# Cross-attention with LayerNorm: slices of x prepared one iteration ahead, and four gaps in the SBUF layout

## The reference

```python
qs = (x @ wq)   ; ks = (ctx @ wk) ; vs = (ctx @ wv)        # split into 16 heads
scores = einsum('bhqd,bhkd->bhqk', qs, ks) / sqrt(32)
scores = where(mask, -inf, scores)
attn = einsum('bhqk,bhkd->bhqd', softmax(scores), vs)
out = attn @ wo + x
return (out - mean(out)) / sqrt(var(out) + 1e-5) * gamma + beta
```

## Time and profile before

| | |
|---|---|
| median of the runs | 677.32 us |
| the profiled execution | 678.04 us, its span in the trace 676.3 us |
| TensorE busy | 616.6 us (91%) |
| VectorE busy | 521.6 us (77%) |
| ScalarE busy | 510.6 us (76%) |
| GpSimd busy | 493.3 us (73%) |
| DMA engines' share | 40.9%, mean 121 GB/s |
| granted clock of TensorE | 0.968 of full speed on average |

### The profile page before, as it was taken

How to read it: one execution, slowest core, us unless ns; L and a number is a source line. 1 busy time by engine, 2 the same in 40 slices (tenths; PEclk the granted TensorE clock), 3 DMA queues, 4 the chain that set the end, 5 groups by cost and what they waited for, 6 DMA issues and landing times.

```text
span 676.3 us, 12773 instructions
## 1 busy us (share of the span) xinstructions
PE 616.6 (91%) x3856; PEld 484.2 (72%) x3856; DVE 521.6 (77%) x1060; ACT 510.6 (76%) x1558; POOL 493.3 (73%) x640
## 2 busy tenths in 40 slices
PE   8999969899898998989899898989989898998995
PEld 6887757777676787767678676767867676777663
DVE  6677757968787786878869687886868878688887
ACT  6788748868787896877779687787868779587851
POOL 4577347867868777786977778697777869667784
PEclk9999979989998998999999899999989999998998
DMA  8522345444544343344434344443434443452102
GB/s 280 160 63 76 103 130 147 119 132 120 136 133 134 102 140 113 116 142 127 139 95 132 100 133 136 116 152 108 131 96 123 138 136 89 130 150 86 44 36 109
DMA packets 60756, 82.02 MB, mean 121 GB/s; under 512 B 22544, under 2 KB 23056, under 8 KB 60688
## 3 DMA queue, kind: packets, MB, share of 16 engines
q1 hardware_dynamic: 60688, 81.21, 40.9%
HBM read 39.53 MB, written 16.78 MB: 83 GB/s over the span
## 4 chain that ended last, share of the span: by engine, by line
PE 57%; DVE 13%; POOL 12%; issue 6%; SPq 5%; ACT 4%; DMA 2%; POOLq 0%; DVEq 0%
PE bank L424 20%; PE bank L523 18%; PE bank L462 6%; PE bank L473 5%; PE bank L496 4%; POOL pn L973 3%; POOL xl L958 3%; DVE pr L782 2%; POOL y L997 2%; DVE nm L788 2%; PE bank L501 2%; SPq L280 2%; PE bank L477 2%; ACT pr L630 2%; POOL pn L975 2%
## 5 line engine op out<-in xcount | busy, mean ns | idle before, releaser
L630 ACT ACTIVATE pr<-pr,nm 128x77 f32<-128x77 f32 x1024 | 270.5, 349 | 59.4 <-DVE nm L788 55.8
L973 POOL TENSOR_TENSOR pn<-pr,rec 128x512 f32<-128x512 f32 x128 | 135.0, 1055 | 126.4 <-DVE rec L797 90.2
L782 DVE SCALAR_TENSOR_TENSOR pr<-msk,bank 128x308 f32<-128x308 uint8 x256 | 109.5, 469 | 83.4 <-PE bank L462 78.1
L424 PE MATMUL bank<-xh,wqh 128*128 128x512 f32 x256 | 108.9, 425 | 43.5 <-POOL xl L958 43.5
L795 DVE TENSOR_REDUCE sm<-pr 128x8 f32<-128x616 f32 x128 | 100.6, 786 | 16.9 <-ACT pr L630 16.3
L424 PE MATMUL bank<-xl,wqh 128*128 128x512 f32 x256 | 106.5, 416 | 0.0
L424 PE MATMUL bank<-xh,wql 128*128 128x512 f32 x256 | 106.0, 414 | 0.0
L788 DVE TENSOR_REDUCE nm<-pr 128x8 f32<-128x616 f32 x128 | 101.8, 795 | 4.4
L462 PE MATMUL bank<-ks,qs 128*128 128x234 f32 (+1 forms) x672 | 103.2, 290 | 2.0 <-DVE pr L782 2.0
L523 PE MATMUL bank<-woh,ah 128*128 128x512 f32 x256 | 103.2, 403 | 1.5 <-DVE al L804 1.4
L601 ACT ACTIVATE ptr<-bank 128x512 f32<-128x512 f32 (+1 forms) x256 | 96.1, 430 | 10.8 <-PE bank L473 10.7
(11 more groups left out here) (85 smaller groups left out, 927.7 us busy)
## 6 DMA issues: line engine op xcount, KB each, us to landing
qs<-qs SPq DMA_DIRECT2D x336, 64.0 KB, 2.0
xraw<-xT SPq DMA_DIRECT2D x58, 256.0 KB, 3.8
xres<-x SPq DMA_DIRECT2D x58, 256.0 KB, 2.7
out<-y SPq DMA_DIRECT2D x56, 256.0 KB, 2.3
ptr<-xT SPq DMA_DIRECT2D x6, 256.0 KB, 9.7
zt<-x SPq DMA_DIRECT2D x6, 256.0 KB, 4.2
out<-zt SPq DMA_DIRECT2D x6, 256.0 KB, 2.0
ks<-khc SPq DMA_DIRECT2D x36, 38.5 KB, 2.0
```

What stands on the lines that cost most here:

```text
L424: last = nc.tensor.matmul(misc_bank(("q", i))[:], w[:, k, m * P:(m + 1) * P], s[:, blk % 2, k, :], start=(k == 0 and n == 0), stop=(k == K ...
L630: last = nc.scalar.activation(s, s, ACT.Exp, bias=nm[:, t % 2, h:h + 1], scale=1.0)
L782: nc.vector.scalar_tensor_tensor(out=pr[:, 4 * g:4 * g + 4, :], in0=msk[:, m % MR, t % 4, :].unsqueeze(1).broadcast_to([P, 4, LK]), scalar ...
L973: nc.gpsimd.tensor_tensor(pn[:, half, 0:4, :].rearrange("p s (e k) -> p (s e) k", e=2), pr[:, hs, 0:KM], rec[:, t % 2, hs].unsqueeze(2).br ...
```

## The change

On SyncE, ScalarE and GpSimd the three steps of a slice are each issued one iteration earlier from iteration 7 on; at the end of iteration 6 each of the three does one slice more than before. TensorE's and VectorE's programs stay as they are. Four unused tensors are declared, and `mhalf` is moved.

```diff
+XDUE = 6
...
         ks = sb("ks", [P, 2, NG, 9, KW], f32r)
+        sb("pad_vm", [P, 16])
         vm = sb("vm", [P, NB, 4, 2, HD])
...
         ident = sb("ident", [P, P])
-        mhalf = sb("mhalf", [P, 1])
+        sb("pad_x", [P, 96])
         xraw = sb("xraw", [P, NX, D])
...
         pr = sb("pr", [P, H, LK])
+        sb("pad_pn", [P, 16])
         pn = sb("pn", [P, 2, 5, P])
...
         msk = sb("msk", [P, MR, 4, LK], u8)
+        mhalf = sb("mhalf", [P, 1])
+        sb("pad_q", [P, 88])
...
             for t in range(T + LAG):                      # SyncE
-                if t >= 1 and t + 9 < 4 * NBLK:
-                    load_slice(t + 9)
+                n = t + 9 + (t > XDUE)
+                if 1 <= t and n < 4 * NBLK:
+                    load_slice(n)
...
                 if t in KS_AT:
                     place_k(*KS_AT[t])
+                if t == XDUE:
+                    load_slice(t + 10)
...
                 if t >= 2:                                # ScalarE
                     keep_pt(t - 2, 1)
-                if 1 <= t and t + 8 < 4 * NBLK:
-                    keep_x(t + 8)
+                n = t + 8 + (t > XDUE)
+                if 1 <= t and n < 4 * NBLK:
+                    keep_x(n)
...
                 exps(t, 1)
+                if t == XDUE:
+                    keep_x(t + 9)
...
                     gain_and_shift(t - LAG - 2)           # GpSimd
-                if t + 8 < 4 * NBLK:
-                    low_x(t + 8)
+                n = t + 8 + (t > XDUE)
+                if n < 4 * NBLK:
+                    low_x(n)
...
                 normalise(t, 0)
+                if t == XDUE:
+                    low_x(t + 9)
```

## The result

The kernel after takes 627.28 us (median of 4 runs, 625.71 to 627.51) against 677.22 us before (4 runs, 676.59 to 677.45). The ratio is 0.9259, 95% interval 0.9243 to 0.9275. The forecast of 630.3 us was 3.0 us too high. The profiled execution took 627.39 us, its span 625.6.

The account below looks back on a forecast made before the run. TensorE, busy 91%, was held mainly by waits for GpSimd's low part of x; 678.04 - 51.2 + 4.2 = 631.0 for the profiled execution, 630.3 us as median, range 622 to 641.

Parts of the forecast that it names:

- the stall: Iterations 3 modulo 4: TensorE's wait for GpSimd's low part of x goes in all 12 blocks, -51.2 us.
- The gaps: Four unused tensors shift operand starts in memory; claimed not to change TensorE's pace, 0 us.
- start-up: Iterations 7 to 9: exponentials wait behind slice 16's late landing, delaying TensorE; +4.2 us, bounds 0 and 7.
- another distance between matmuls: Sign of being wrong: 512-column matmuls on TensorE no longer 233 ns apart from start to start.
- the half clock: TensorE's slow stretches behind 8 of the 12 waits go with them; 8 x 1.57 = 12.5 us of the gain.
- A third plain iteration in a row: Rival: it does not hold in the blocks, 0.8 us come back in each; 640 us, chance 0.14.
- the residual of tile 1: VectorE, start-up: ends at 105.1, so `project_o(2)`, which writes the bank it reads, starts 3.6 us later.
- `low_q(12)`: Iteration 8: frees the bank of `project_q(13)` late, an estimated 0.6 us.
- The first rival: Both operands on a multiple of 128 bytes bring 512-column matmuls from 233 to 213 ns; 620 us, chance 0.07.
- GpSimd's loop: Plain iterations: GpSimd has no idle time, repeats every 8.00 us against TensorE's 8.03, and holds if matmuls get faster.
- The last iterations: From iteration 56 on: same instructions at the same distance, 0, give or take 1.6 us for one slow clock stretch.

Follow-up runs that it names:

- e10: Kernel after with weights at 160 and x and attention at 416 modulo 512, some other gaps changed too; 623.21 us in one execution.
- e6: Kernel after with x and attention at 0 modulo 512 instead of 384, weights still at 128; 629.79 us, ratio 0.9313 to the kernel before.
- the later hand-over: Kernel after with the slices ahead from iteration 10 on instead of 7; 622.56 us, ratio 0.9211 to the kernel before.

## Why the prediction was right, step by step

The term that makes up nearly all of the change, the stall, was right for the reason given. The gaps were put at nothing and were not nothing, and in the start-up the size came out by a path that was not the one followed. One of the prediction's own signs of being wrong came: another distance between matmuls.

*The stall.* Right in mechanism and size. The slices alone took the 12 blocks from 477.93 to 426.77 us, 51.2 less; predicted were 426.7 and 51.2. The trace of before has the 8 slow stretches in these blocks that the prediction had worked out from the mean clock; with the slices alone none is left there, so the half clock went with the waits. How the 51.2 divide was less exact: 38.7 us were called waiting, and the earlier trace rows has 35.9. A third plain iteration in a row held at 8.04, so that rival fell.

*Start-up.* The size was right for the slices alone: iteration 8 started at 105.11 instead of 100.90, +4.2, as predicted, and iteration 10 still had it (124.61 against 120.40). The path was another than I followed, and that the size fits to 0.1 us is luck. I had `project_o(2)` wait for the residual of tile 1 and added 0.6 us for `low_q(12)`; neither shows as a wait of TensorE. In fact it waited for ScalarE's `keep_pt`, which stood behind the two late slices and frees the bank of the transposes. ScalarE in order of time after, the answer to the earlier trace rows:
```profile
92.05 0.63 ACT L610 ACTIVATE xh<-xraw 128x512 fp32r<-128x512 f32 x1 [7.77 <-DMA xraw<-xT]
92.59 0.58 ACT L610 ACTIVATE qs<-bank 128x512 fp32r<-128x512 f32 x1
93.07 0.76 ACT L610 ACTIVATE ptr<-bank 128x512 f32<-128x512 f32 x2
99.25 0.63 ACT L610 ACTIVATE xh<-xraw 128x512 fp32r<-128x512 f32 x1 [5.43 <-DMA xraw<-xT]
99.79 0.80 ACT L662 ACTIVATE y<-z,rs 128x512 f32<-128x512 f32 x1
100.49 2.09 ACT L639 ACTIVATE pr<-pr,nm 128x77 f32<-128x77 f32 x8
102.49 0.73 ACT L610 ACTIVATE ptr<-bank 128x512 f32<-128x512 f32 x2
```
The exponentials start at 100.49 (I had 101.4), and the transposes at 103.37 wait for the `ptr` copy at 102.49. I read only what stands behind `keep_x(16)` and left out `keep_pt(5, 1)` and `keep_pt(6, 0)`, which stand behind the slices in the same queue. Iteration 8 starts 4.6 us behind the start of `keep_x(16)`, in the kernel after (99.25) as with the slices alone (100.50); the slice came 1.25 us earlier in the kernel after, and so that one has +3.0 and not +4.2. There the pause was followed by another slow stretch of the clock, 0.50 from 104.20 to 107.62, and that is why its iteration 8 takes 9.54 us: its `project_o` starts its matmuls 0.44 us apart.
```profile
104.97 0.65 PE L532 MATMUL bank<-woh,ah 128*128 128x512 f32 x1
105.41 0.63 PE L532 MATMUL bank<-wol,ah 128*128 128x512 f32 x1
```

*The gaps.* The term that was mis-sized: 0 predicted, about -5 us measured. The distances say the same: 3.5 and 4.1 ns less in the two projections, 768 times each, are 5.8 us if TensorE sets the pace throughout. The range from 622 to 641 had room for a term of this size. From the two groups in the earlier trace rows I concluded that no start matters, since they ran at one pace with opposite operands off the multiple. Both have the same difference of 96 between their operands' starts, modulo 256, and it is the difference that counts, so the comparison could not show it. The first rival had the sign, but of its 20 ns per matmul 3.5 to 4.1 came, and 4.4 and 5.8 in e10; what the rest of the distance above 213 ns is, no run shows. Its condition, both operands on a multiple of 128, was not the one either: e6 has it and 232.6 ns.

*GpSimd's loop.* I had its 8.00 us as a floor for a plain iteration. It was not: TensorE runs at 7.96 after and at 7.89 in e10. GpSimd needs longer than that (8.04) and falls back, but three plain iterations in a row did not use up its lead.

*The last iterations.* From iteration 56 to the end of the span 97.47 us before, 97.06 after, 95.9 with the slices alone, where the clock had one slow stretch instead of three: within the 1.6 that was allowed.

The sum for the profiled execution after: +3.0 to iteration 8, -53.3 in the 12 blocks, -0.4 behind them, together -50.7 against 678.04 - 627.39 = 50.65 measured.

What stays open is why the difference of the two starts matters. That it does is shown, in the table; the cause behind it is not. Nor was e10's layout run together with the later hand-over.

## What to carry to other kernels

An engine that waits once in a block for the last of several operands prepared in its own iteration gains the wait and the slow clock behind it when the preparation goes one iteration ahead at equal work; make the switch where the queue that feeds it has caught up, since the operation that is moved ahead stands in front of everything else in its engine's queue. Before calling a margin of another engine a floor, count for how many iterations in a row it must hold. When two rows are to show that a property does not matter, check that they differ in it in every form, the difference between two operands included.

## What the hardware showed that I had not expected

In this kernel the pace of float32r matmuls of 512 columns at full clock depends on where moving and stationary operand start against each other in a partition, modulo 256 bytes: 228.0 to 230.2 ns at a difference of 0, 232.6 at 128, 233.4 to 233.9 at 96, and 229.9 and 233.6 at 64 and 192. Of the operands, moving the weights alone changed it as much as moving x and attention (from 232.6 to some 230 in both cases).
